# Channel order of the projected heads: one store where two or more were, and another order of the start

## The reference

```python
def _L0_attn_ref(x, w_qkv, w_out):          # x = layernorm of the stream, as (1, 8*256 tokens in its chunks, 128)
    qkv = x @ w_qkv                          # 16 heads of 8 channels
    # chunks of W = 64 queries see the chunk before and their own, causal
    scores = jnp.einsum('bhcqd,bhckd->bhcqk', qc, kcat) / HD ** 0.5
    attn = jax.nn.softmax(jnp.where(mask, scores, -jnp.inf), axis=-1)
    return heads_joined(attn @ vcat) @ w_out

x = x + _L0_attn_ref(_layernorm(x), L0_attn_w_qkv, L0_attn_w_out)
x = x + _L0_xattn_ref(_layernorm(x), ctx_1024, ctx_1024, mask, Wq, bq, Wk, bk, Wv, bv, Wo, bo)   # 16 heads, 256 keys
x = x + _L0_ffn_ref(_layernorm(x), w1, conv_w, conv_b, w2)    # quantised linear, depthwise conv of 3, silu, quantised linear
```

## Time and profile before

| what | us |
| --- | --- |
| median of 3 runs | 321.65 |
| lowest, highest | 319.15, 323.3 |
| the profiled execution | 319.63 |
| its span in the trace | 317.9 |
| TensorE busy | 283.1 (89% of the span) |
| VectorE busy | 223.8 (70%) |
| ScalarE busy | 165.2 (52%) |
| GpSimd busy | 142.3 (45%) |

### The profile page before, as it was taken

The page is one execution under the profiler, slowest core; times in us unless marked ns, Lnnn a source line. Parts: engine busy times, 40 slices in busy tenths (PEclk is TensorE's granted clock), DMA queues, the critical chain, the costliest instruction groups (busy, mean ns, idle before and its releaser), DMA issues.

```text
span 317.9 us, 8708 instructions
## 1 busy us (share of the span) xinstructions
PE 283.1 (89%) x3310; PEld 181.0 (57%) x3315; DVE 223.8 (70%) x562; ACT 165.2 (52%) x329; POOL 142.3 (45%) x219
## 2 busy tenths in 40 slices
PE   6519295999999999999999999999988988999993
PEld 2405164777787777777566655556544454544541
DVE  7846271458667666988787778687775359999674
ACT  2311023454565565557776776677677762333432
POOL 7754397274685684674967530000026303442000
PEclk9978676899999999999999999999999999999999
DMA  5465649457584663554645645300000000000001
GB/s 172 87 153 121 165 94 255 117 114 211 176 237 119 194 158 91 143 136 93 161 108 129 168 92 144 107 3 3 1 2 1 2 1 2 26 17 18 22 22 33
DMA packets 36376, 30.98 MB, mean 97 GB/s; under 512 B 4812, under 2 KB 32364, under 8 KB 36208
## 3 DMA queue, kind: packets, MB, share of 16 engines
q1 hardware_dynamic: 35464, 30.00, 37.7%
q10 hardware_dynamic: 872, 0.44, 0.5%
HBM read 16.53 MB, written 13.63 MB: 95 GB/s over the span
## 4 chain that ended last, share of the span: by engine, by line
PE 65%; DVE 11%; SPq 11%; issue 4%; ACT 4%; DMA 3%; ACTq 1%; POOL 0%; DVEq 0%
SPq L1193 9%; PE ps L338 9%; PE ps L303 8%; PE ps L268 7%; PE ps L403 7%; PE ps L351 5%; PE ps L314 4%; PE ps L286 3%; PE ps L309 2%; PE ps L378 2%; ACT probs L598 2%; PE ps L362 2%; PE ps L272 2%; PE ps L276 2%; DVE probs L839 2%
## 5 line engine op out<-in xcount | busy, mean ns | idle before, releaser
L759 DVE TENSOR_REDUCE negm<-ps 128x2 bf16<-128x512 f32 (+1 forms) x192 | 123.7, 690 | 60.4 <-PE ps L276 27.1
L598 ACT ACTIVATE probs<-ps 128x512 f32<-128x512 f32 x192 | 105.8, 608 | 42.8 <-PE ps L314 30.3
L303 PE MATMUL ps<-QT,KT 98*128 98x512 bf16 x128 | 47.5, 382 | 4.3 <-ACT probs L598 4.1
L268 PE MATMUL ps<-KT,QT 97*128 97x256 bf16 x256 | 47.5, 272 | 0.5
L403 PE MATMUL ps<-tapw,xqT 128*128 128x512 f32 x96 | 44.1, 592 | 0.3 <-issue 0.2
L268 PEld LDWEIGHTS ps<-KT,QT 97*128 97x128 bf16 x256 | 23.8, 98 | 14.9 <-DVE negm L759 2.8
L338 PE MATMUL ps<-probs,V 128*32 128x256 f32 x512 | 30.9, 382 | 0.7 <-ACT probs L598 0.7
L1006 POOL TENSOR_TENSOR ve<-mv,eps 128x2 f32<-128x2 f32 x8 | 1.6, 197 | 64.0 <-DVE mv L796 64.0
L1061 POOL TENSOR_SCALAR_AFFINE_SELECT probs<-probs 128x512 f32<-128x512 f32 x32 | 21.2, 663 | 14.9 <-ACT probs L598 14.9
L636 ACT ACTIVATE probs<-ps 128x512 f32<-128x512 f32 x16 | 9.6, 598 | 33.2 <-PE ps L403 31.0
L403 PEld LDWEIGHTS ps<-tapw,xqT 128*128 128x128 f32 x96 | 18.2, 190 | 15.0 <-issue 14.3
(11 more groups left out here) (137 smaller groups left out, 503.4 us busy)
## 6 DMA issues: line engine op xcount, KB each, us to landing
stack_parts<-high SPq DMA_DIRECT2D x64, 96.0 KB
QT<-stack_parts SPq DMA_DIRECT2D x32, 192.0 KB
KT<-stack_parts SPq DMA_DIRECT2D x16, 384.0 KB
stack_parts<-mid SPq DMA_DIRECT2D x64, 64.0 KB, 2.3
stack_parts<-low SPq DMA_DIRECT2D x64, 32.0 KB, 1.9
CT<-in_ctx_t_dram SPq DMA_DIRECT2D x1, 1024.0 KB, 7.6
out_dram<-probs SPq DMA_DIRECT2D x16, 64.0 KB, 1.5
tapw<-in_taps_dram SPq DMA_DIRECT2D x1, 768.0 KB, 6.3
```

The lines of the kernel that those rows point to most:

```text
L268: last = nc.tensor.matmul(o[:, j * S:(j + 1) * S], QT[r, s, j, pr, t * P:(t + 1) * P], KT[r, s, pr, :], start=True, stop=True)
L303: last = nc.tensor.matmul(o.rearrange("p (j q) -> p j q", j=2), KT[r, s, pr, kt * P:(kt + 1) * P], QT[r, s, :, pr, :], start=True, stop=True)
L598: nc.scalar.activation(probs[:, k, :], bank(n % 3), ACT.Exp, scale=SCALE).then_inc(s_exp, 1)
L759: nc.vector.tensor_reduce(dst, src, AX.X, ALU.max, negate=True).then_inc(m_max, 1)
```

## The change

The channels are ordered by channel, then head, then pair. Both heads of a pair now lie within one run of 128 partitions, and the DRAM tensor has 12 slots of 128 rows: 0 to 5 for Q, 6 to 11 for K. A unit's stores are five: high of Q to slots 0 to 2, high of K to 8 to 10, mid of Q to 4 and 5, mid of K to 7 and 11, and low of both in one (slots 3 and 6). The loads into QT write every second partition of 96, from rows in steps of 8 KB. The host's order of the weight columns follows. Beside that, V is zeroed and given its ones by ScalarE instead of VectorE, TensorE's filler matmuls are four instead of eight and stand behind the projection of unit 4, VectorE normalises units 4 and 5 ahead of the rests of units 2 and 3, and SyncE's order in the start is another, without its wait for the first row of maxima.

```diff
-Q_SLOTS = ((0, 1, 2), (3, 4), (5,))
-K_SLOTS = ((1, 3, 5), (0, 4), (2,))
-STORED = 64
+TWICE, LOW_AT = (((0, 3, 1), (8, 11, 1)), ((4, 6, 1), (7, 12, 4))), (3, 7, 3)
+STORED = (32, 32, 16)
...
-        parts = nc.dram_tensor("stack_parts", (4, 2, 2, 6, 64, S), BF16, kind="Internal").ap()
+        parts = nc.dram_tensor("stack_parts", (4, 12, P, S), BF16, kind="Internal").ap()
...
                 x_turn(4, bank(6)).then_inc(xT_ps, 1)
                 pe.wait_ge(xT_sb, 4)
-                turn_over(8)
                 x_turn(5, bank(7)).then_inc(xT_ps, 1)
                 qk_project(4, bank(5))
+                pe.wait_ge(xT_sb, 6)
+                turn_over(4)
...
+                def v_slot(e):
+
+                    act.wait_ge(s_ws, 1)
+                    nc.scalar.activation(V[:, e].rearrange("p a m c -> p (a m c)"), ones[:, 0:1].to_broadcast([P, 3 * PAIRS * 4 * VW]),
+                                         ACT.Copy, scale=0.0).then_inc(v_made, 1)
+                    act.wait_ge(v_made, 2 * e + 1)
+                    nc.scalar.copy(V[:, e, :, 0:4:3, HD], ones[:, 0:2 * 3 * PAIRS].rearrange("p (a m) -> p a m", m=2)).then_inc(v_made, 1)
+
                 ox_copy(0, bank(6), S, 2 * S)
                 high_copy(0, bank(0))
                 ox_copy(1, bank(7), S, 2 * S)
                 high_copy(1, bank(1))
+                v_slot(0)
                 ox_copy(2, bank(6), S, 2 * S)
                 ox_copy(3, bank(7), S, 2 * S)
                 high_copy(2, bank(3))
                 v_copy(0, bank(2))
+                ox_copy(4, bank(6), S, 2 * S)
                 high_copy(3, bank(4))
-                ox_copy(4, bank(6), S, 2 * S)
                 ox_copy(5, bank(7), S, 2 * S)
                 raw_copy(4, bank(5))
+                v_slot(1)
                 m_copy(0, bank(BX, BF16))
...
                 x_stats(5)
-                link(nc.vector.memset(V[:, 0], 0.0))
-                link(nc.vector.memset(V[:, 0, :, 0:4:3, HD:HD + 1], 1.0))
+                link(nc.vector.memset(bias3[:], 0.0))
+                link(nc.vector.memset(onesb[:], 1.0))
+                normalise(4)
+                normalise(5)
                 rest_make(2, bank(3))
                 rest_make(3, bank(4))
-                normalise(4)
-                normalise(5)
-                link(nc.vector.memset(V[:, 1], 0.0))
-                link(nc.vector.memset(V[:, 1, :, 0:4:3, HD:HD + 1], 1.0))
-                link(nc.vector.memset(bias3[:], 0.0))
-                link(nc.vector.memset(onesb[:], 1.0))
...
                 def store(u, part):
-                    src, done = ((high, high_done), (mid, mid_done), (low, low_done))[part]
-                    sp.wait_ge(done, u + 1)
-                    for j in range(2):
-                        for n, slots in enumerate((Q_SLOTS[part], K_SLOTS[part])):
-                            step = slots[1] - slots[0] if len(slots) > 1 else 1
-                            sp.dma_start(parts[u % 4, n, j, slots[0]:slots[-1] + 1:step].rearrange("s p t -> p s t"),
-                                         src[64 * j:64 * j + 64, n, u % 2 * S:(u % 2 + 1) * S].unsqueeze(1).to_broadcast(
-                                             [64, len(slots), S])).then_inc(part_out[part][u % 2], 16)
+                    sp.wait_ge((high_done, mid_done, low_done)[part], u + 1)
+                    t = (high, mid, low)[part][:, :, u % 2 * S:(u % 2 + 1) * S]
+                    kept = parts[u % 4]
+                    if part < 2:
+                        for n, (lo, hi, step) in enumerate(TWICE[part]):
+                            sp.dma_start(kept[lo:hi:step].rearrange("s p t -> p s t"),
+                                         t[:, n].unsqueeze(1).to_broadcast([P, 3 - part, S])).then_inc(part_out[part][u % 2], 16)
+                    else:
+                        lo, hi, step = LOW_AT
+                        sp.dma_start(kept[lo:hi:step].rearrange("s p t -> p s t"), t).then_inc(part_out[2][u % 2], 16)
 
                 def load(u):
...
-                        sp.dma_start(QT[48 * j:48 * j + 48, u % SLOTS, j].rearrange("p r t -> p (r t)"),
-                                     parts[u % 4, 0, j].rearrange("s (c r) t -> (s c) (r t)", r=PAIRS)).then_inc(st_in[u % SLOTS], 16)
+                        sp.dma_start(QT[j:ROWS:2, u % SLOTS, j].rearrange("p r t -> p (r t)"),
+                                     kept[0:6].rearrange("s (c j r) t -> (s c) j (r t)", j=2, r=PAIRS)[:, j]
+                                     ).then_inc(st_in[u % SLOTS], 16)
                     sp.dma_start(KT[0:ROWS, u % SLOTS].rearrange("p r t -> p (r t)"),
-                                 parts[u % 4, 1].rearrange("j s (c r) t -> (j s c) (r t)", r=PAIRS)).then_inc(st_in[u % SLOTS], 16)
+                                 kept[6:12].rearrange("s (x r) t -> (s x) (r t)", r=PAIRS)).then_inc(st_in[u % SLOTS], 16)
...
                 store(0, 1)
                 store(0, 2)
                 store(1, 0)
+                store(1, 1)
                 load(0)
-                store(1, 1)
                 store(1, 2)
+                store(2, 0)
+                load(1)
                 query_row(2)
-                store(2, 0)
                 store(2, 1)
-                load(1)
+                store(3, 0)
                 store(2, 2)
-                for part in range(3):
-                    store(3, part)
+                store(3, 1)
+                load(2)
+                store(3, 2)
                 query_row(3)
-                sp.wait_ge(m_row[0], 16)
-                load(2)
                 load(3)
...
-    order = _np.array([(2 * pr + j) * HD + c for j in range(2) for c in range(HD) for pr in range(PAIRS)])
+    order = _np.array([(2 * pr + j) * HD + c for c in range(HD) for j in range(2) for pr in range(PAIRS)])
```

More of the change, by code:

```diff
@@ L189, in decoder_kernel @@
         rows_q = [sem(f"ones_row_in{i}") for i in range(SLOTS)]
-        s_zero = sem("query_slots_zeroed")
+        s_zero, v_made = sem("query_slots_zeroed"), sem("value_slots_made")
         s_ws, s_wps, s_wsc, s_pf = sem("w_sums"), sem("w_sums_spread"), sem("w_scales"), sem("pool_ffn_steps")
@@ L210, in stack_in @@
             return 16 * sum(4 if is_cross(e) else 3 for e in range(u % SLOTS, u + 1, SLOTS))
-        Q_READY, V_READY, V_ALL = 1, 3, 7
+        Q_READY, CONST_ALL = 1, 3
         PC_IDENT, PC_ALL = 3, 9
@@ L526, in _ @@
                     max_unit_mms(n)
-                pe.wait_ge(s_dc, V_ALL)
+                pe.wait_ge(s_dc, CONST_ALL)
                 pe.wait_ge(v_sb, 1)
@@ L564, in high_copy @@
                     if u >= 2:
-                        act.wait_ge(part_out[0][u % 2], STORED)
+                        act.wait_ge(part_out[0][u % 2], STORED[0])
                     nc.scalar.copy(high[:, :, u % 2 * S:(u % 2 + 1) * S], src.rearrange("p (n t) -> p n t", n=2)
@@ L581, in v_copy @@
                     if u < 2:
-                        act.wait_ge(s_dc, (V_READY, V_ALL)[u])
+                        act.wait_ge(v_made, 2 * (u + 1))
                     else:
@@ L1030, in high_part @@
                     g.wait_ge(raw_done, u - 3)
-                    g.wait_ge(part_out[0][u % 2], STORED * (u // 2))
+                    g.wait_ge(part_out[0][u % 2], STORED[0] * (u // 2))
                     nc.gpsimd.tensor_copy(half_of(high, u), raw[:, :, u % 2 * S:(u % 2 + 1) * S]).then_inc(high_done, 1)
@@ L1041, in mid_part @@
                     if u >= 2:
-                        g.wait_ge(part_out[1][u % 2], STORED * (u // 2))
+                        g.wait_ge(part_out[1][u % 2], STORED[1] * (u // 2))
                     nc.gpsimd.tensor_copy(half_of(mid, u), raw[:, :, u % 2 * S:(u % 2 + 1) * S]).then_inc(mid_done, 1)
@@ L1047, in low_part @@
                     if u >= 2:
-                        g.wait_ge(part_out[2][u % 2], STORED * (u // 2))
+                        g.wait_ge(part_out[2][u % 2], STORED[2] * (u // 2))
                     nc.gpsimd.tensor_tensor(half_of(low, u), raw[:, :, u % 2 * S:(u % 2 + 1) * S], half_of(mid, u),
@@ L1197, in load @@
                 def load(u):
                     for part in range(3):
-                        sp.wait_ge(part_out[part][u % 2], STORED * (u // 2 + 1))
+                        sp.wait_ge(part_out[part][u % 2], STORED[part] * (u // 2 + 1))
+                    kept = parts[u % 4]
                     for j in range(2):
-                        sp.dma_start(QT[48 * j:48 * j + 48, u % SLOTS, j].rearrange("p r t -> p (r t)"),
-                                     parts[u % 4, 0, j].rearrange("s (c r) t -> (s c) (r t)", r=PAIRS)).then_inc(st_in[u % SLOTS], 16)
+                        sp.dma_start(QT[j:ROWS:2, u % SLOTS, j].rearrange("p r t -> p (r t)"),
+                                     kept[0:6].rearrange("s (c j r) t -> (s c) j (r t)", j=2, r=PAIRS)[:, j]
+                                     ).then_inc(st_in[u % SLOTS], 16)
```

## The result

The changed kernel took 309.14 us, the median of four runs (307.68 to 310.91), against 321.29 before (319.15 to 323.3): a ratio of 0.9625, 95% interval 0.954 to 0.971. It is 12 us faster. The profiled run took 307.68 us; its span fell from 317.9 to 305.9. Measured again beside other kernels, it came to 0.960 and 0.953 of the kernel before, with medians of 310.13 and 307.76. A run over 1.5% above the fastest of its kernel is counted in the medians and ranges here but not in the ratios: two of six of the changed kernel in each of these two groups, two in run 5, one in run 10, and in run 3 one of 407.6 us, whose granted clock was 0.651.

The account below looks back on a forecast made before the run. SyncE's queue of store issues was taken to bound the start, TensorE the middle; iteration 1 at 46.0 instead of 58.63 gives 12.6 us, so 307.0 profiled, 309.0 by the median, 308.5 said; range 303.5 to 313.5, by itself 305 to 312.

Parts of the forecast that it names:

- Issues: SyncE's queue in the start: 0.65 us a store, 28 stores dropped, 18.2 us of 36 saved, not yet the gain.
- The DMA engines' service of stores: Prologue: stores at 202 GB/s, 3.9 us a unit, so the DMA engines, not SyncE, pace it after the change.
- the quicker figure set beside the rows: Estimate from the Trainium skill's page, about 358 GB/s: a unit's stores would take 2.2 us.
- the first rival: DMA engines keep up and SyncE's issues pace: low(2) lands 26.3, gain 17.5 us, 304 us; chance 0.20.
- Beat 0: TensorE's first score beat of unit 0 comes at about 32.0 us instead of 43.84, 11.8 us earlier.
- GpSimd as the next limit: GpSimd's list sets the first probabilities-times-V group: keep done at 44.0, TensorE waits about 3 us, iteration 1 at 46.0.
- "Nothing is booked" in the middle: From 60 to 240 us the kernel stays bound by TensorE; no gain or loss counted there.
- in time: Maxima's row on ScalarE's queue, written at about 27.6 us, has over 4 us to land, against a store's longest 3.8.
- V on ScalarE: Zeroing V by ScalarE in the start takes 1.8 us, bounds 1.34 to 4.9, in gaps of its list.
- The rest of the start's order: Fillers cost between 0 and 1 us; SyncE's dropped wait for the first maxima's row worth 0.
- Rival 4: Slower: writing every second partition makes Q's loads crawl; at 12 us a load, 351 us; chance 0.03.
- Rival 3: A store issue with twice the packets takes twice as long, only 5 us of SyncE go: 316 us; chance 0.05.

Follow-up runs that it names:

- run 5: Changed kernel with GpSimd's zeroing of slot 5 and the mask row moved behind the keeps of iterations 0 and 1: 305.42 us, ratio 0.948.
- run 10: Changed kernel with V zeroed by VectorE again, nothing else changed back: 307.0 us against 307.76 of the changed kernel beside it.
- run 3: Changed kernel with twelve stores a unit, each slot stored by its own transfer from 128 partitions: 314.85 us, ratio 0.977.
- run 6: Changed kernel with SyncE waiting for the landed row of maxima before each bulk load: 306.92 us, ratio 0.955.
- run 1: The new channel order with its five stores and its loads alone, the start's order as in the kernel before: 309.01 us, ratio 0.962.
- run 9: Changed kernel with slot 5 behind the keeps, mask row between two keeps, rows ahead of bulk loads, and SyncE's old start order: 303.36 us, ratio 0.942.
- run 4: Changed kernel with SyncE's list of the start as before the change: 305.7 us, ratio 0.950.
- run 2: Old layout with twelve stores a unit, everything else of the start in the changed kernel's order: 322.92 us, ratio 1.003.

## Why the prediction was right

The total was forecast at 308.5 (305 to 312 by itself) and measured at 309.14; the profiled run at 307.0 and 307.68. The mechanism was right: a queue of issues in front of TensorE, then GpSimd's list. Three terms were off, and that the total came within 1 us is in part luck: the stores served quicker than forecast brought GpSimd's keep 2.7 us forward, a lower clock of TensorE behind it took 1.3 of that back, and the late rows took 2.1.

- *SyncE.* Issues: 0.65 us a store was forecast, the median is 0.49; a load of three took 1.8 us (1.45 forecast); load(0) went out at 14.29 (15.05 forecast).
- *The DMA engines' service of stores* was mis-sized: I took the 202 GB/s of 64-partition stores for those of 128, "as before per byte". Measured about 280, so a unit's stores take 2.8 us of full DMA time instead of 3.9; the quicker figure set beside the rows was 2.2. low(2) landed by 28.8, between the 31.4 of the forecast and the 26.3 of the first rival; the share over 17 to 37 us was 0.69, not over 0.85. So the first rival's sign came, but only a part of its effect: the gain up to iteration 1 was 14.0, where it had 17.5. Run 3 shows that the service goes with the partitions and not with the count.
- *Beat 0* at 31.36 (32.0 forecast), from maxima of unit 0 at 21.05 (21.2) and of unit 1 at 26.92 (27.4).
- *GpSimd as the next limit*: mask row done at 35.43 (38.1), keep done at 41.33 (44.0), TensorE's wait 2.30 (about 3), iteration 1 at 44.60 (46.0). Its chain of 5.85 us was 5.9. From the keep to iteration 1 it took 3.3 us where 2.0 was forecast: the granted clock was 0.50 from 41.2 to 44.5 us, which the forecast had nothing for; in the second profile, at full clock, it took 1.7 from the group on. Run 5 confirms the cause: without the two operations iteration 1 starts at 41.69.
- *"Nothing is booked" in the middle*, and the row of maxima "in time": this step failed. I had followed the first row only, and bounded its landing by a store's longest, 3.8 us. The rows' own record before was longer: the one issued at 48.97 took 6.6 us to land, in the stretch with a share of 0.99, and nobody waited for it, as iteration 1 began at 58.63. After, iterations 1 to 3 are 2.1 us longer, 1.75 of it in three waits for rows; run 6 bears out that SyncE's bulk loads are the cause. In the other two profiles it was one wait of 0.73 or 0.60.
- *V on ScalarE*: 1.49 and 0.27 us (1.8 forecast), in the gap ahead of unit 2's copy as said. The rest of the start's order had been booked at 0 to 1 us; runs 1, 9 and 10 find it at 0.
- *Rival 4*, Q's loads into every second partition: not seen. No wait for a stack is left after 60 us.
- *Rival 3*: the stores' issues didn't lengthen with the packets. Those of the loads did grow, from 0.42 to 0.58 us, with the same bytes from a tensor of another shape.

So 14.0 - 2.1 = 11.9 (the spans say 12.0) stands where 12.6 - 0 was forecast.

## What to carry to other kernels

Where a queue of small transfers leads the chain, count its issues, but look also at how many partitions each transfer spans: here twelve stores of 128 partitions, each shorter to issue and quicker to serve, already gave about 7 of the 12 us, and five gave the rest. Once that queue is short, another order in it gained nothing that could be measured (runs 1, 4 and 9); shortening the next list behind it (here GpSimd's), with the rows ahead of the bulk loads, did, and gave a better kernel than both, 303.55 us (0.9435). A move is finished only when its neighbour in time on the other engines has been looked at: the mask row cost 1.3 us in one place and nothing one keep earlier. And one profile is one execution: two more of the same kernel had one late row instead of three.

## What the runs showed that I had not expected

- Stores from 64 partitions ran at 202 GB/s at full share, from 128 at 288 with the same number of transfers and packets (278 with five transfers a unit and a load among them).
- Issuing a store took SyncE 0.62 us from 64 partitions and 0.43 from 128 (medians of the high stores in runs 2 and 3).
- A small transfer on another engine's queue is slowed by bursts: 8 KB landed in 1.8 us at the least and in 5.0 to 5.8 beside a load of a stack, the context and the next stores; before the change one had taken 6.6 without anyone waiting.
- VectorE's cast took 2.27 us beside a GpSimd operation that began 0.02 us earlier, and 0.54 us elsewhere.
- One and the same 2.3 us wait of TensorE was followed by no, three, four or ten us at the lower clock (1.2 of 2.4 GHz).
